# Moving three chunks of the first expert block from before the last softmax to behind it

## The reference

```python
x = x + attn(layernorm(x))             # q, k, v = x @ W; elu(q)+1, elu(k)+1; V = q (k^T v) / (q . sum k)
x = x + xattn(layernorm(x), ctx_1024)  # q, k, v with biases; softmax(q k^T / 16) v over 77 context rows
x = x + ffn(layernorm(x))              # shared expert + the two best of 8 experts, weighed

def ffn(xf):
    shared = new_gelu(xf @ Wfc_s + bfc_s) @ Wproj_s + bproj_s      # 256 -> 1024 -> 256
    probs = softmax(xf @ Wr); topk_p, topk_i = top_k(probs, 2)     # topk_p divided by its sum
    for e in range(8):
        routed += (new_gelu(xf @ Wfc[e] + bfc[e]) @ Wproj[e] + bproj[e]) * gate[:, e]
    return shared + routed
```

## Time and profile before

| What | us |
|---|---|
| Median of 3 runs | 764.33 |
| Lowest and highest of them | 763.49 and 4344.75 |
| The profiled execution, its own time | 764.01 |
| Its span, from the first to the last instruction | 762.2 |
| What lies around the span | 1.8 |

### The profile page before, as it was taken

One profiled execution on the slowest core, in us unless ns is written; L12 is line 12 of the kernel. 1 busy time (PEld: TensorE's weight loads), 2 busy tenths in 40 slices (PEclk: granted clock), 3 DMA queues, 4 the chain that ended last, 5 costly groups with the idle time before them and its releaser, 6 DMA issues.

```text
span 762.2 us, 21931 instructions
## 1 busy us (share of the span) xinstructions
PE 733.3 (96%) x6887; PEld 615.8 (81%) x6887; DVE 590.8 (78%) x1800; ACT 413.0 (54%) x937; POOL 229.6 (30%) x221
## 2 busy tenths in 40 slices
PE   3999999999889999999999999999999999999995
PEld 1777677787678888888888888888888888888783
DVE  4589999998878988998776766677666767777774
ACT  3567767666777667667533333333333334555552
POOL 2110110111012076666113323333223333333333
PEclk9999999999999999999999999999999999999999
DMA  5667898965372479998634444444344434344431
GB/s 147 176 160 176 217 216 205 201 163 106 75 187 71 126 241 304 297 300 265 188 52 64 66 71 70 65 59 65 66 72 65 58 66 71 70 75 71 70 69 22
DMA packets 163123, 97.29 MB, mean 128 GB/s; under 512 B 105260, under 2 KB 158408, under 8 KB 163016
## 3 DMA queue, kind: packets, MB, share of 16 engines
q1 hardware_dynamic: 149720, 78.81, 42.1%
q0 software_dynamic: 13296, 17.09, 12.8%
HBM read 38.73 MB, written 36.15 MB: 98 GB/s over the span
## 4 chain that ended last, share of the span: by engine, by line
PE 89%; DVE 4%; DMA 2%; SPq 1%; issue 1%; ACT 1%; POOL 0%; POOLq 0%; DVEq 0%; ACTq 0%
PE bank_kv L1422 9%; PE bank_kv L1423 9%; PE bank_kv L1424 9%; PE bank L1399 6%; PE bank L1401 6%; PE bank L1400 6%; PE bank_st L1401 6%; PE bank_st L1399 6%; PE bank_st L1400 6%; PE bank_kv L1520 5%; PE bank_kv L1415 5%; PE bank_st L1499 4%; PE bank_st L1480 3%; PE bank L1550 2%; PE bank_kv L1416 2%; PE bank L1457 1%
## 5 line engine op out<-in xcount | busy, mean ns | idle before, releaser
L748 ACT ACTIVATE expert_buffers<-bank_st,bias_columns 128x256 f32<-128x256 f32 (+1 forms) x248 | 108.2, 437 | 134.2 <-DVE expert_buffers L1018 73.9
L1422 PE MATMUL bank_kv<-w_parts,expert_buffers 128*128 (+1 forms) x656 | 179.2, 273 | 1.4 <-DVE expert_buffers L1018 1.4
L1424 PE MATMUL bank_kv<-w_parts,expert_buffers 128*128 (+1 forms) x656 | 179.1, 273 | 0.0
L1423 PE MATMUL bank_kv<-w_parts,expert_buffers 128*128 (+1 forms) x656 | 179.1, 273 | 0.0
L748 ACT ACTIVATE expert_buffers<-bank,bias_columns 128x256 f32<-128x256 f32 (+1 forms) x246 | 107.3, 437 | 130.5 <-PE bank L1401 100.4
L1018 DVE SCALAR_TENSOR_TENSOR expert_buffers<-expert_buffers 128x256 f16<-128x256 f32 x328 | 138.8, 424 | 22.0 <-ACT expert_buffers L754 12.4
L1017 DVE TENSOR_SCALAR expert_buffers<-expert_buffers 128x256 f16<-128x256 f32 x260 | 82.2, 316 | 63.2 <-ACT expert_buffers L748 56.3
L669 POOL DMA_INDIRECT out<-expert_buffers,token x71 | 118.2, 1664 | 17.1 <-issue 16.8
L1401 PE MATMUL bank_st<-expert_buffers,w_parts 128*128 128x256 f16 (+1 forms) x368 | 87.1, 248 | 0.0
L1399 PE MATMUL bank<-expert_buffers,w_parts 128*128 128x256 f16 (+1 forms) x368 | 86.9, 248 | 0.2 <-issue 0.2
L1401 PE MATMUL bank<-expert_buffers,w_parts 128*128 128x256 f16 (+1 forms) x368 | 87.0, 248 | 0.0
(11 more groups left out here) (224 smaller groups left out, 1564.6 us busy)
## 6 DMA issues: line engine op xcount, KB each, us to landing
rows_by_expert<-w_parts SPq DMA_DIRECT2D x12, 795.0 KB, 5.1
stage_w<-in_L_ffn_Wfc SPq DMA_DIRECT2D x9, 512.0 KB, 5.6
stage_w<-in_L_ffn_Wproj SPq DMA_DIRECT2D x9, 512.0 KB, 5.3
rows<-in_x SPq DMA_DIRECT2D x16, 256.0 KB, 4.9
x_residual<-rows SPq DMA_DIRECT2D x16, 256.0 KB, 2.8
expert_buffers<-x_residual SPq DMA_DIRECT2D x16, 256.0 KB, 3.0
out<-expert_buffers SPq DMA_DIRECT2D x16, 256.0 KB, 4.4
w_parts<-in_L_ffn_Wfc SPq DMA_DIRECT2D x7, 512.0 KB, 5.2
```

The costliest lines, as they stand in the source:

```text
L748: act.activation(spare[:, at], hid_of(c)[:, 0:width(G)], ACT.Gelu_apprx_tanh, bias=bias, scale=UNSCALE).then_inc(s["gelu_done"], 1)
L1422: pe.matmul(y, g[:, 0, tile(t)], w_hi, start=f == 0 and t == 0, stop=False, skip_group_check=True)
L1423: pe.matmul(y, g[:, 0, tile(t)], w_lo, start=False, stop=False, skip_group_check=True)
L1424: op = pe.matmul(y, g[:, 1, tile(t)], w_hi, start=False, stop=f == FC - 1, skip_group_check=True)
```

## The change

Chunks 3, 4 and 5 of the first block change their place on ACT and DVE, and the order on PE is changed to suit. On ACT, gelu 3 to 5 leave step 17, and with them the `exp_table()` of that step; they now stand behind `copy_prob(15)`. On DVE, splits 3 to 5 leave step 17; split 3 stands ahead of `add_context(15)`, split 4 ahead of `sums`, split 5 behind `variances`. On PE, `weigh_values(15)` moves up behind `route_logits(13)`, and down 3 moves down behind it. No arithmetic changes.

```diff
--- before.py
+++ after.py
@@ -776,9 +776,6 @@
                 if i == LAST + 1:
                     gelu(0, E)
                     gelu(1, E)
-                elif i == LAST + 2:
-                    gelu(3, E)
-                    gelu(4, E)
                 if live(i + 1) and i != -1:
                     norm_first(i + 1)
                 if live(i + 1) and i != -1:
@@ -813,9 +810,6 @@
                 if i == LAST + 1:
                     gelu(2, E)
                     exp_table()
-                elif i == LAST + 2:
-                    gelu(5, E)
-                    exp_table()
                 if i in SPLIT_STEPS:
                     convert_shared(*SPLIT_STEPS[i])
                 if i == 0:
@@ -847,6 +841,9 @@
             exp_scores(LAST)
             high_third(LAST - 1)
             copy_prob(LAST)
+            gelu(3, E)
+            gelu(4, E)
+            gelu(5, E)
 
             def convert_last(half, w, stage, name, done):
 
@@ -1069,8 +1066,6 @@
                         .then_inc(s["ctxT_lo"], 1)
                 if i == LAST + 1:
                     split(0)
-                elif i == LAST + 2:
-                    split(3)
                 if live(i - 3):
                     add_context(i - 3)
                 if live(i + 2) and i <= 0:
@@ -1082,8 +1077,6 @@
                     sums(i, 2, i - 3, True)
                 if i == LAST + 1:
                     split(1)
-                elif i == LAST + 2:
-                    split(4)
                 if live(i + 1) and i != -1:
                     low(0, i + 1)
                 if sums_of:
@@ -1101,8 +1094,6 @@
                                              ALU.add, ALU.subtract).then_inc(s["key_ready"], 1)
                 if i == LAST + 1:
                     split(2)
-                elif i == LAST + 2:
-                    split(5)
                 if live(i):
                     got(dve, "reluq_ready", i)
                     dve.scalar_tensor_tensor(qfeatT, expq, 1.0, qfeatT, ALU.min, ALU.add).then_inc(s["qfeat_ready"], 1)
@@ -1138,9 +1129,12 @@
             layer_norm(2, LAST - 1)
             low_third(LAST - 1)
             invert_sum(LAST)
+            split(3)
             add_context(LAST)
+            split(4)
             sums(LAST + 3, 2, LAST, True)
             variances(LAST + 3, [(2, LAST)])
+            split(5)
 
             def then(op):
                 route_count[0] += 1
@@ -1573,12 +1567,12 @@
                 step(i)
             scores(LAST)
             up(0, 0, E, 6)
-            down(0, 0, E, 3)
             turn_prob(LAST)
             route_logits(LAST - 2)
+            weigh_values(LAST)
+            down(0, 0, E, 3)
             up(0, 0, E, 7)
             down(0, 0, E, 4)
-            weigh_values(LAST)
 
             experts = {}
```

## The result

The changed kernel takes 765.28 us (median of 15 runs, 764.23 to 766.99), the kernel before 764.33 (15 runs); the ratio is 1.0016 with a 95% interval of 1.0008 to 1.0023, so 0.6 to 1.8 us slower. That is inside the predicted range of 763.3 to 767.8; the direction was right, and the size, +0.95 against a forecast of +2.0, was half. A part of the working was wrong, and that part holds the lesson: the table loads that I counted as worthless are worth 1.3 us. They only looked covered in the one execution that I had read, because PE ran there at its lower clock.

What follows compares the result with a forecast made beforehand. PE, busy 96% of the span, was taken as the bound. A lag of 1.4 us plus 1.5 for a clock fall, less 0.9 taken up by two waits, left +2.0 on 764.01: 766.0 us, range 763.3 to 767.8.

Steps and rivals of the forecast that it cites:

- The table changes: removed, worth nothing: ACT, 204 to 212 us: two table loads and a dummy go, 2.8 us, but nobody waited; gain 0, at most 0.1.
- the splits off DVE in step 17: worth nothing on the path: DVE, step 17: three splits of 0.43 us go; `add_context(14)` can start 0.3 us earlier, but PE then idles longer behind it.
- The whole is wrong: Signs against the forecast: Exp earlier than 211.5, down 3 before 215.5, or new waits for splits behind 240.
- The wait added at down 3: PE behind `weigh_values(15)`: idles 1.7 us until split 3 ends; down 3 starts at about 216.2.
- The lag and how much comes back: PE reaches down 6 1.4 us late; waits at 227.45 and 238.68 take up part, leaving +0.6 to +1.0, say 0.8.
- The clock term: TensorE's clock falls to half for 3.4 us behind the 211.7 to 216.2 stretch, costing PE 1.5 us; total becomes +2.0.
- The drain of 1.38 us: The skill's drain on top of a 1.28 us load, 2.66 per switch; the forecast saw none in the trace.
- The sum: Whole kernel: the profiled execution's 764.01 us + 2.0 = 766.0.
- rival 2: Table changes held ACT and the new wait is hidden: PE gains 1.9 us, 762.1, or 761.2 if ACT bounds; chance 0.10.
- rival 1: Lag alone, the clock stays: 764.01 + 0.8 = 764.8 us; chance 0.35.
- Rival 3: Lead of gelus and splits isn't rebuilt; 14 further shared blocks each repeat a 0.45 us wait: 770.3 us; chance 0.05.

Runs made afterwards that it cites:

- e2: The kernel before with Tanh in place of Gelu in chunks 0 to 5, so five table changes become one: 762.92 us, ratio 0.9978.
- r9: The kernel before with only DVE's splits moved in step 17, split 3 behind the variances, 4 and 5 behind the keys' low halves: 762.16 us, ratio 0.9971.
- e4: The changed kernel with 5 unread matmuls added ahead of turn_prob and 13 ahead of down 3: 763.36 us, ratio to before 0.9991.
- e6: The changed kernel with 13 unread matmuls added ahead of down 3 alone: 763.48 us, ratio to before 0.9991.
- e3: The changed kernel with Tanh in place of Gelu in chunks 0 to 5, one load left ahead of gelu 6: 762.85 us, ratio to before 0.9980.

## Why the prediction was right or wrong

- **"The table changes: removed, worth nothing" failed**, and with it "the splits off DVE in step 17: worth nothing on the path". I put the gain at 0 and at most 0.1; it is 1.3 us in A (e2; 1.2 in r9, which only takes DVE's splits out of the way). The row on which I leaned was right (ACT waits 1.09 us for PE at 208.42), but it was read behind a stretch in which PE ran at 0.50 of its clock. I used that stretch to price the fall, and didn't ask what it hid: a fall there makes A 1.3 us longer than PE's work needs (8.11 in e4, 6.80 in e6), and in the changed kernel's profile it is not there. The path that I missed goes over DVE, whose split 3 waits for ACT's copy behind the load, with `add_context(14)` in the queue behind it. It stood in the trace that I read:

```profile
206.56 0.43 DVE L1018 SCALAR_TENSOR_TENSOR expert_buffers<-expert_buffers 128x256 f16<-128x256 f32 x1 [1.78 <-ACT expert_buffers L754]
```

The gain for `add_context(14)` I priced at 0.3 us from this execution, in which PE's slow `weigh_values(14)` was about as late as the split; at full clock it is 1.6 (3.07 against 4.64).

- **Two of my own signs of a wrong prediction came true.** "The whole is wrong" stood there for an Exp ahead of 211.5 and for a down 3 ahead of 215.5; they came at 209.01 and 213.47. Of that, 1.4 us are the earlier `turn_prob(14)` of this execution, the rest is the 1.3 us of A. The signs were set on the times of one execution, where intervals were called for.
- **The wait added at down 3: right.** It is 3.69 us behind `turn_prob(15)` against a forecast of 3.7, a wait of 1.64; e3 shows that the table load makes it.
- **The lag and how much comes back: right in kind**, a little under the forecast: 0.5 to 0.6 against 0.6 to 1.0. The waits at 227.45 and 238.68 are gone, as said.
- **The clock term: right in kind and near in size.** It falls in all 37 runs, costs 1.2 to 1.5 in B where I had 2.0 - 0.8 = 1.2, and goes when the gap is filled. The Trainium skill (TensorE: Matmul & The Clock Gate, A second HAM failure mode) tells of a kernel whose clock goes up and down because PE "micro-idles between MM groups frequently enough". This case agrees in kind: ahead of the fall, PE idled 0.72, 0.18 and 1.64 us between its groups.
- **The drain of 1.38 us that the Trainium skill adds to a table load** (ScalarE: Activation LUTs, What ACT_TABLE_LOAD costs) doesn't show here: `copy_prob` ends at 210.64, gelu 3 starts at 211.96, and the load itself fills 1.28 of these 1.32 us.
- **The sum.** B is +1.8 to +2.1, my +2.0 almost to the tenth. A is -1.3, my 0. That leaves +0.7 where I had +2.0. The forecast of 766.0 was 0.7 over the measured median, because one half of rival 2 (the table changes held something up) was true together with the forecast, and I had set them against each other; its other half, a hidden wait at down 3, was not. That the time is in the range is in part owed to the range's width: a term of 1.3 us was missing, and the range spans 4.5. Its stated reasons give less, 764.3 (rival 1 less half a microsecond) to 767.4 (764.33 + 3.1); both measured medians lie in that too.
- **Rival 3 (slower for good) did not happen**: no wait for a split behind 217 us up to the short blocks.

## What to carry to other kernels

Before a wait or a load is called covered, ask whether the cover itself is normal: look at the granted clock over the covering stretch, and at a second execution. And what a slow instruction costs is set by who is queued behind its result on the next engine: moving three small splits on DVE behind the work that others wait for brought as much as doing without the table loads (1.2 against 1.3 us of A), and without a new gap in PE.

## What the runs showed of the hardware that I had not expected

- The clock fell at a gap of PE of 1.64 us: in the three profiles of the changed kernel the fall begins between 0.5 us ahead of the gap's end and 0.6 us behind it, with PE busy for 1.93 of the 3.9 us before (209.00 to 212.90 in the first profile), and none of its 37 runs is without a fall. With 13 matmuls in the gap, 22 of 23 are. The stretch of 3.73 us with 1.82 busy ahead of 202 us is as empty, and yet the kernels e3, e4, e6 and r9, which all have it, run without any fall 40 times of 42.
- A few matmuls into an unused half bank keep the clock up, and cost nothing where PE would wait anyway: down 3 starts 3.69 us behind `turn_prob(15)` with them and without (e6).
- Kernels that are the same up to step 16 reach `turn_prob(14)` at 200.8 to 202.4 us in their profiled executions, so two single executions differ by more than this change is worth. All of it arises in PE's first 24 matmuls. These are the rows before, and behind them those of the changed kernel:

```profile
12.01 5.28 PE L1520 MATMUL bank_kv<-w_parts 128*128 128x512 f16 x12 [12.01 <-DMA w_parts<-w_parts]
17.09 1.87 PE L1550 MATMUL bank<-w_parts 128*128 128x256 f16 x12
```

```profile
12.05 4.17 PE L1514 MATMUL bank_kv<-w_parts 128*128 128x512 f16 x12 [12.05 <-DMA w_parts<-w_parts]
16.07 1.47 PE L1544 MATMUL bank<-w_parts 128*128 128x256 f16 x12
```

The same matmuls, begun at the same time, end 1.4 us apart, and from the next row on to `turn_prob(14)` it is 183.5 to 183.6 us in every profile. That would fit a lower clock that lasts longer at the start of one execution than of another, but the profile's clock column doesn't show it there, so the cause stays open.
